# A decoder layer on one core: x, context and two weights come transposed from the host, and the context is split by ScalarE and GpSimd a step ahead

## The reference

```python
# self part: scores of x with itself, small probabilities taken out
scores = einsum('btd,bsd->bts', x, x) / sqrt(256)
probs  = softmax(scores)
sparse = where(probs < 0.01, 0, probs); vac_sum = sum(where(probs < 0.01, probs, 0))
sparse = sparse / (sum(sparse) + 1e-9)
x = layernorm(x + sparse @ x + 0.01 * broadcast(vac_sum) @ W.T)
# cross attention: 16 heads of 16 over the context
q = x @ Wq + bq;  k = ctx @ Wk + bk;  v = ctx @ Wv + bv
att = softmax(where(mask, -1e15, q @ k.T / 4)) @ v
x = layernorm(x + att @ Wo + bo)
# 8 linear experts, the best 2 by softmax(x @ Wr): sum of p_e * (x @ Wi[e] @ Wo[e])
x = layernorm(x + experts(x))
```

## Time and profile before

| | us |
|---|---|
| median of 3 runs | 902.17 (901.38 to 902.78) |
| the profiled execution | 903.45 |
| its span in the trace | 901.7 |
| PE, DVE, ACT, POOL busy | 870.3, 741.9, 656.2, 137.5 |
| one pass in the middle (x1T to x1T) | 26.16 |

### The profile page before, as it was taken

How to read it: one execution, slowest core, us unless ns; L and a number is a source line. 1 busy time by engine, 2 the same in 40 slices (tenths; PEclk the granted TensorE clock), 3 DMA queues, 4 the chain that set the end, 5 groups by cost and what they waited for, 6 DMA issues and landing times.

```text
span 901.7 us, 26330 instructions
## 1 busy us (share of the span) xinstructions
PE 870.3 (97%) x8264; PEld 767.8 (85%) x8264; DVE 741.9 (82%) x2808; ACT 656.2 (73%) x2033; POOL 137.5 (15%) x261
## 2 busy tenths in 40 slices
PE   4799999999999999999999999999999999999985
PEld 3688889889988888898988889888888888888874
DVE  3557888888888888888888888888888888888765
ACT  2388777787877777787777788777777877777760
POOL 1101111111111111111111111111111111111101
PEclk9999999999999999999999999999999999999998
DMA  9532333443333443433334433333443343433300
GB/s 265 149 80 71 98 98 101 111 97 95 88 91 96 104 107 93 107 84 93 97 100 105 102 90 92 97 98 98 102 107 94 83 106 88 103 92 89 84 12 11
DMA packets 84776, 87.42 MB, mean 97 GB/s; under 512 B 18576, under 2 KB 80640, under 8 KB 84640
## 3 DMA queue, kind: packets, MB, share of 16 engines
q1 hardware_dynamic: 84640, 85.74, 37.3%
HBM read 23.13 MB, written 3.67 MB: 30 GB/s over the span
## 4 chain that ended last, share of the span: by engine, by line
PE 91%; DVE 3%; issue 2%; ACT 1%; DMA 1%; SPq 1%; POOL 0%; POOLq 0%; DVEq 0%; ACTq 0%
PE psum L1054 21%; PE psum L919 18%; PE psum L910 11%; PE psum L935 10%; PE psum L996 8%; PE psum L989 7%; PE psum L978 3%; PE psum L1010 3%; PE psum L972 2%; PE psum L1032 2%; PE psum L961 2%; PE psum L1003 1%; PE psum L954 1%; PE psum L966 1%; DMA wout_sb<-in_wout 1%
## 5 line engine op out<-in xcount | busy, mean ns | idle before, releaser
L459 ACT ACTIVATE probs<-masked,nmax 112x375 f32<-112x375 f32 x512 | 313.8, 613 | 49.0 <-DVE nmax L590 45.1
L590 DVE CUSTOM_DVE_ANT_0 masked<-psum,mask_add 112x375 f32<-112x375 f32 x512 | 277.8, 543 | 63.1 <-PE psum L910 54.4
L487 ACT ACTIVATE probsT<-psum 125x336 f32<-125x336 f32 x512 | 229.4, 448 | 85.2 <-PE psum L919 84.9
L919 PE MATMUL psum<-const_sb,probs 112*125 112x112 f32 x1536 | 250.6, 272 | 0.0
L919 PEld LDWEIGHTS psum<-const_sb,probs 112*125 112x125 f32 x1536 | 236.6, 188 | 15.1 <-issue 6.1
L910 PE MATMUL psum<-k_stack,q_stack 96*112 96x376 f32 x512 | 204.4, 399 | 2.7 <-issue 2.4
L410 POOL TENSOR_SCALAR var_eps<-moments 112x1 f32<-112x1 f32 x96 | 21.3, 222 | 752.4 <-DVE moments L785 351.4
L604 DVE SCALAR_TENSOR_TENSOR mix<-psum,gate,mix 112x256 f32<-112x256 f32 x224 | 108.1, 482 | 17.6 <-PE psum L1054 2.9
L1054 PE MATMUL psum<-we_hi,x_hi 128*112 128x512 f32 x256 | 108.5, 424 | 1.8 <-DVE mix L604 1.8
L910 PEld LDWEIGHTS psum<-k_stack,q_stack 96*112 96x112 f32 x512 | 90.1, 176 | 21.3 <-issue 8.6
L459 ACT ACTIVATION_READ_ACCUMULATOR probs<-masked,nmax 112x1 f32 x512 | 101.6, 198 | 0.0
(11 more groups left out here) (122 smaller groups left out, 1540.3 us busy)
## 6 DMA issues: line engine op xcount, KB each, us to landing
k_stack<-k_hi SPq DMA_DIRECT2D x256, 93.8 KB, 2.2
q_stack<-q_hi SPq DMA_DIRECT2D x256, 56.0 KB, 2.0
ctx_sb<-in_context SPq DMA_DIRECT2D x32, 375.0 KB
k_stack<-k_lo SPq DMA_DIRECT2D x128, 93.8 KB, 2.2
q_stack<-q_lo SPq DMA_DIRECT2D x128, 56.0 KB, 2.0
x_sb<-in_x SPq DMA_DIRECT2D x32, 112.0 KB, 2.2
out_dram<-out_sb SPq DMA_DIRECT2D x32, 112.0 KB, 2.4
wi_sb<-in_wi SPq DMA_DIRECT2D x2, 1024.0 KB, 9.2
```

Of the source, the lines that this page charges most:

```text
L459: nc.scalar.activation(probs[:, n % RING, :], masked[:, n % RING, :], ACT.Exp, bias=nmax[:, n:n + 1], scale=-1.0, accum_out=probs_sum[a[1] ...
L487: nc.scalar.activation(probsT[:, i % TRING, :], psum[0:KP, T_BANKS[i % 2], 0:KT * TOK], ACT.Copy).then_inc(probsT_copied, 1)
L590: nc.vector.tensor_tensor_reduce(masked[:, n % RING, :], psum[0:TOK, S_BANKS[n % 2], 0:KEYS], mask_add[k][:, :, :].rearrange("t j p -> t ( ...
L919: mm = nc.tensor.transpose(psum[0:KP, T_BANKS[n % 2], j * TOK:(j + 1) * TOK], probs[:, n % RING, j * KP:(j + 1) * KP], ident[0:TOK, 0:TOK])
```

## The change

What it does:

- The host also passes x transposed (`x_T`), and it passes the context, W and the experts' first weights only transposed. The kernel loads them as they are; the context tile becomes 128 x 2 x 376, with a last column of zeros.
- c0, c1 and xT leave `USES`, T0 to T3 leave `WEIGHT_USES`, the transposes of W leave the prologue. Slot and bank of all others stay.
- ctx_hi is now one ScalarE instruction from SBUF over 752 columns, in slot 1, for the batch of the `self` stage (a pass earlier than before), and ctx_lo one GpSimd instruction, between the mask and the second layer norm's 1/sqrt. Both have two buffers.
- The scale of the self scores moves from the xT copy into the exponent (SELF_SCALE is now 1/16), and VectorE scales the maximum in one more one-column instruction (self_nmax).
- The tiles for the experts' weights hold half of them (4 experts). The second half is issued in pass -1, behind the stacking DMAs of that pass and a wait for E3.
- The mask is read in its own order, no longer in the permuted one of the context rows.

```diff
-SELF_SCALE = DIM ** -0.25
+SELF_SCALE = DIM ** -0.5
-USES = [("x1T", 0, "G1"), ("c0", 0, "G2"), ("c1", 0, "G0"), ("m0", 1, "G1"), ("rb", 1, "O"),
-        ("xT", 2, "G0"), ("qT", 2, "G2"), ("K0", 3, "G0"), ("Wo", 4, "G1"), ("Sc", 5, "G2"),
+USES = [("x1T", 0, "G1"), ("m0", 1, "G1"), ("rb", 1, "O"), ("qT", 2, "G2"), ("K0", 3, "G0"), ("Wo", 4, "G1"), ("Sc", 5, "G2"),
...
-WEIGHT_USES = [("T0", 1, "G1"), ("E0", 3, "G1"), ("T1", 7, "G0"), ("T2", 8, "G2"), ("E1", 9, "G0"),
-               ("E2", 10, "G1"), ("T3", 12, "G2"), ("E3", 14, "G0")]
+WEIGHT_USES = [("E0", 3, "G1"), ("E1", 9, "G0"), ("E2", 10, "G1"), ("E3", 14, "G0")]
...
+                sp.dma_start(xT[k][:, :, :], x_T[row(at)]).then_inc(x_in[k], 16)
+                sp.dma_start(x_sb[k][:, :], x[row(at)]).then_inc(x_in[k], 16)
...
                     load_x(shift(at, 3))
+                    if due(act_self.to("ctx_hi", p)):
+                        sp.wait_ge(act_self.sem, act_self.to("ctx_hi", p))
+                    if due(pool_self.to("ctx_lo", p)):
+                        sp.wait_ge(pool_self.sem, pool_self.to("ctx_lo", p))
+                    load_context(shift(at, 3))
...
                 if it == FIRST:
-                    expert_weights()
+                    expert_weights(0)
+                if it == FIRST + 1:
+                    sp.wait_ge(pe_weights.sem, pe_weights.to("E3", p))
+                    expert_weights(1)
...
+                if own:
+                    pool.wait_ge(act_self.sem, act_self.to("ctx_hi", s))
+                    nc.gpsimd.tensor_tensor(
+                        ctx_lo[k][:, :, :], ctx_sb[k][:, :, :], ctx_hi[k][:, :, :].bitcast(fp32), ALU.subtract)\
+                          .then_inc(pool_self.did("ctx_lo"), 1)
                 if join:
                     inverse_deviation(2, "join", o)
...
-                    if proj and n == 0:
-                        for c in range(DC):
-                            act.wait_ge(pe_proj.sem, pe_proj.to(f"c{c}", p))
-                            nc.scalar.activation(
-                                ctx_hi[:, c, 0:KEYS], bank_of[f"c{c}"][:, 0:KEYS], ACT.Copy)\
-                                  .then_inc(act_proj.did(f"ctx_hi{c}"), 1)
+                    if own and n == 1:
+                        act.wait_ge(ctx_in[k], turn(s, 1))
+                        if due(pe_proj.to("V2", a)):
+                            act.wait_ge(pe_proj.sem, pe_proj.to("V2", a))
+                        nc.scalar.activation(
+                            ctx_hi[k][:, :, :].rearrange("p c t -> p (c t)"),
+                            ctx_sb[k][:, :, :].rearrange("p c t -> p (c t)"), ACT.Copy)\
+                              .then_inc(act_self.did("ctx_hi"), 1)
...
-                    if n == 1 and proj:
-                        for c in range(DC):
-                            dve.wait_ge(act_proj.sem, act_proj.to(f"ctx_hi{c}", p))
-                            nc.vector.tensor_tensor(
-                                ctx_lo[:, c, 0:KEYS], bank_of[f"c{c}"][:, 0:KEYS],
-                                ctx_hi[:, c, 0:KEYS].bitcast(fp32), ALU.subtract)\
-                                  .then_inc(dve_proj.did(f"ctx_lo{c}"), 1)
...
+                            nc.vector.tensor_scalar(
+                                self_nmax[:, :], self_top[:, :], SELF_SCALE, None, ALU.mult)\
+                                  .then_inc(dve_self.did("self_nmax"), 1)
```

More of the change, by code:

```diff
@@ L132, in previous_use, with decoder_layer @@
     return None
-def decoder_layer(nc, x, context, mask, attn_w, wq, bq, wk, bk, wv, bv, wo, bo, wr, wi, wout,
+def decoder_layer(nc, x, x_T, context_T, mask, attn_w_T, wq, bq, wk, bk, wv, bv, wo, bo, wr, wi_T, wout,
                   consts, out):
@@ L295, in decoder_layer @@
         for j in range(EXPERTS_PER):
-            taken[f"T{j}"], taken[f"E{j}"] = (act_steps, f"wiT{j}"), (dve_steps, f"we_lo{j}")
+            taken[f"E{j}"] = (dve_steps, f"we_lo{j}")
         def settle(eng):
@@ L341, in _, with expert_weights @@
                   .then_inc(weights_in, 16)
-            def expert_weights():
-                for part in range(EXPERTS // EXPERTS_PER):
-                    e = slice(part * EXPERTS_PER, (part + 1) * EXPERTS_PER)
-                    for dst, src in ((wi_sb, wi), (wout_sb, wout)):
-                        sp.dma_start(dst[:, e, :, :], src[e].rearrange("e (c p) n -> p e c n", p=128))\
-                          .then_inc(wi_in[part], 16)
+            def expert_weights(part):
+                e = slice(part * EXPERTS_PER, (part + 1) * EXPERTS_PER)
+                for dst, src in ((wiT, wi_T), (wout_sb, wout)):
+                    sp.dma_start(dst[:, :, :, :], src[e].rearrange("e (c p) n -> p e c n", p=128))\
+                      .then_inc(wi_in[part], 16)
             def iteration(at, it):
@@ L366, in iteration @@
                     settle(sp)
-                    load_context(shift(at, 2))
+                    load_mask(shift(at, 2))
                 if active("moe", it - 1):
@@ L488, in iteration @@
                                              ACT.Copy).then_inc(probsT_copied, 1)
-                    if own and n == 2:
-                        act.wait_ge(pe_self.sem, pe_self.to("xT", s))
-                        nc.scalar.activation(
-                            xT[:, :, :].rearrange("p c t -> p (c t)"), bank_of["xT"][:, 0:DC * TOK],
-                            ACT.Copy, scale=SELF_SCALE).then_inc(act_self.did("xT"), 1)
                     if attn and 0 < n < HEADS:
@@ L555, in _ @@
                 nc.vector.memset(k_stack[k][:, :, :, KEYS:KEYS_EVEN].bitcast(fp32), 0.0)
-            for part in (ctx_hi, ctx_lo):
-                nc.vector.memset(part[:, :, KEYS:KEYS_EVEN].bitcast(fp32), 0.0)
             nc.vector.memset(ones[:, :], 1.0).then_inc(setup_dve, 1)
```

149 lines of the change are left out of this document (60 added, 89 removed).

## The result

The changed kernel takes **932.68 us** (928.33 to 932.96, 4 runs) against 901.77 us before (900.85 to 902.78, 4 runs): ratio 1.033 (1.030 to 1.036), 3.3% slower. Forecast were 890.7 us, with 881 to 899 as the range. The profiled execution took 932.96 us, its span is 931.2 us.

What follows compares the result with a forecast made beforehand. PE's instruction stream was taken as the bound. xT 5.3, c0 and c1 2.9, pass 1 0.8 and the prologue 2.5 sum to 11.5 us off: 892.0 on the profiled execution's scale, 890.7 as median; range 881 to 899.

Steps and rivals of the forecast that it cites:

- the window: 413.15 to 415.35 us in a pass, when GpSimd's ctx_lo would run; conflict with VectorE there was counted as nothing.
- The last rival: GpSimd's ctx_lo and VectorE shut each other out, VectorE becomes the bound: slower, 931 us; chance 0.06 with milder forms.
- the one long x_bo: GpSimd's x_bo in the prologue, 1463 ns against 736 elsewhere, while VectorE splits wk and wv: cited against the move.
- c0 and c1, 0.10 of 0.64 us: Context transposes leaving PE: 0.10 of 0.64 us a pass won, as m0 waits for ScalarE's x1T copy; 2.9 us in all.
- xT, 0.19, a pass: Transposes of x leaving PE: 0.19 us a pass won in full in passes 2 to 29, 5.3 us.
- GpSimd's ctx_lo, 2.2 us: Length taken for the subtraction moved to GpSimd behind the mask, hidden as long as it doesn't disturb VectorE.
- The prologue: First passes: x1 later, scores earlier, that gain given back by late expert weights; 2.5 us won, between 5 won and 2 lost.
- the late weights: Second half of the expert weights, issued at about 37.6 us, lands at 47.0; E0 of pass 0 waits until then.
- The sum: All terms together: 11.5 us off, 892.0 us on the profiled execution's scale, 890.7 as the forecast median.
- The chance of 0.88 for faster: Chance of a time below 900.4 us: 0.76 for the forecast plus 0.12 for the rival without m0's wait.

Runs made afterwards that it cites:

- ctx_lo late: Changed kernel with GpSimd's ctx_lo moved behind x1_bo and a wait for VectorE's vacuum: 889.54 us, ratio 0.985 to the kernel before.
- K0 as cover: Changed kernel with ctx_lo late on GpSimd, and K0 put ahead of m0 in slot 1: 881.92 us, ratio 0.979 to the kernel before.
- three versions: Changed kernel with ctx_lo on VectorE (891.57 us), with ctx_lo late on GpSimd (889.54), or with the mask waiting for out_sb (889.62).

## Why the prediction was wrong

By its own steps:

- **"In the window ... VectorE runs instructions that read PSUM and one SBUF operand; the first that reads two SBUF operands is q_lo ... I count nothing": this step failed,** in two ways. The term was put at nothing, and it is 1.57 us a pass (27.38 - 25.81), 42 us in 27 passes. The window was laid over ctx_lo alone, 413.15 to 415.35, and out_sb had been over since 412.73; but a queued ctx_lo holds out_sb from before its recorded start. And VectorE's work was sorted by its number of SBUF operands alone: out_sb has one input tensor, but input and result are both in SBUF. The Trainium skill (SBUF — State Buffer, section Who interferes with whom), named in the forecast, counts a two-port mode as well as two inputs, and out_sb behaves as such. That it runs in that mode is inferred from its pace: gate_a, also a tensor_scalar with two values per row, takes 288 ns for 8 columns and out_sb alone some 410 for 256, half a nanosecond a column, where the two-input subtraction wk_lo takes 677 ns for 512 columns and wr_lo 176 for 16, one nanosecond a column. Instructions that read PSUM kept their lengths beside ctx_lo, as the forecast said; that shows where the mask waits for out_sb (masked 0.54, mix 0.48 us), for in the changed kernel none of them ran beside it.
- **The last rival came true**, with 931 us against 932.7, and 27.3 us against 27.38 for the pass. It had 0.06, with the clue already in the rows: the one long x_bo. Its mechanism was right but the working wasn't. It took 4.3 us for ctx_lo, which takes 1.77, and priced the hold by VectorE's busy time (decides from 2.9 us on), by which the measured hold, 3.03 us in place of 0.41, would have cost nothing; VectorE is busy for 24.62 of 27.38 us, so it never became the bound. The price is a delay: out_sb stands in front of a masked head that PE's next score matmul waits for, and only 1.43 us of its length are covered. VectorE's busy time, forecast to fall by 26 us, rose by 45.6 with the hold and fell by 19.7 without it (722.2 with ctx_lo late). That the number came out so near is luck.
- **c0 and c1, 0.10 of 0.64 us, and xT, 0.19, a pass: right.** The forecast for a pass was 25.87; without the hold it is 25.81. The idle time before m0, released by ScalarE's x1T, is there: 0.27 us in PE's row (forecast 0.3 to 0.5). With K0 as cover the mean pass is 25.47, so the transposes were worth 26.16 - 25.47 = 0.69 of the 0.83 taken at face value.
- **GpSimd's ctx_lo, 2.2 us: it takes 1.77.** The estimate of 1.6 us that the forecast gave from the Trainium skill (GPSIMD Engine Reference, section Performance versus the Vector engine) was nearer. ScalarE's cast takes 0.83 us and, as forecast, delays nothing.
- **The prologue:** the late weights held E0 of pass 0 as forecast, at 48.22 us (forecast 47.0), after 5.50 us of idle time (forecast 3). x1 of pass -2 came at 15.66 us, 1.3 later than before (forecast 1.8). What the step left out is that PE runs slowly behind such a wait (last section).
- **The sum** of these steps, 890.7, is what the change gives once out_sb isn't held: 889.5 to 891.6 in three versions. The chance of 0.88 for faster was too high for a sum with one unpriced operation on a shared port.

## What to carry to other kernels

When work moves to GpSimd, list every VectorE instruction that runs from the start of the GpSimd instruction *in front of* the moved one, and treat each one that lies wholly in SBUF as held until the moved one ends, if that is a large one (here from 632 columns on); then look at what is queued behind it and count the delay from there, not the busy time. The cures are cheap where the work isn't urgent: another slot, one wait that lets VectorE go first, or here pieces of 188 or 376 columns in place of 752 (all of them small: a small piece in front of a large one doesn't help). And removed work is only worth what the next wait lets through: put a product that waits for nothing into the gap.

## What the runs showed of the hardware

- **A queued GpSimd instruction holds VectorE before its own recorded start.** The Trainium skill (SBUF — State Buffer, section SBUF: two separate sides) says that whichever starts first gets the shared port pair for its whole instruction. By the records it is not so here: out_sb started 1.11 us before ctx_lo and yielded to it, and the mask, which started before out_sb, let it through in 0.60 us. Where a piece of ctx_lo was the earlier one the rule holds: out_sb took 1.87 us beside 752 columns and 1.07 beside 376, each to 0.15 us behind their end.
- **The size of the queued pieces decides**, with a jump between 504 and 632 columns of two fp32 inputs: 1.29 against 2.78 us in three passes of four. A 632 behind a 120 holds as well, four pieces of 188 don't.
- **VectorE's two-input work is held too.** In the prologue of the changed kernel x_cas, 467 ns in its median, meets ctx_lo (start, length):

```profile
11.11 1.77 POOL L439 TENSOR_TENSOR ctx_lo<-ctx_sb,ctx_hi 128x752 fp32r<-128x752 f32 x1 [10.28 <-DMA bo_row<-in_bo]
11.26 1.89 DVE L753 SCALAR_TENSOR_TENSOR x_cas<-w_sum,vac_scaled,x_sb 112x256 f32<-112x256 f32 x1
```

- **A wait of PE costs again after it.** E0 of pass 0 took 1.89 us before; after 5.50 us of idle time it takes 3.75. The granted clock is 0.50, the 1.2 GHz level, from 48.2 to 50 us and 0.57 in the mean of the next 5 us, before it is back at 1.00, the 2.4 GHz level. From the changed kernel, first the row in order of time, then the stretches (columns as in the earlier trace rows):

```profile
48.22 3.75 PE L999 MATMUL psum<-wout_sb,wiT 128*128 128x256 f32 x8 [5.50 <-DMA wout_sb<-in_wout]
```

```profile
48.20:50.00 1.80, 1.78 (x4) 1.50 (x5) 0.00 (x0) 0.00 (x0) 0.00 (x0) 0.50 0.04 15
50.00:55.00 5.00, 5.00 (x23) 4.55 (x22) 2.50 (x8) 2.09 (x6) 0.00 (x0) 0.57 0.00 0
55.00:60.00 5.00, 5.00 (x53) 4.55 (x53) 4.02 (x18) 4.86 (x16) 0.00 (x0) 1.00 0.39 93
```
